# Attention with one-pass softmax: how the row-maximum units of a head group are dealt out over the score steps

## What is computed

```
c_kv   = x @ W_dkv.T                                   # 64 latent channels
q_lat  = einsum('bhtd,hdl->bhtl', q, k_eff)            # 16 heads
attn   = einsum('bhtl,bsl->bhts', q_lat, c_kv) / sqrt(16)
attn   = softmax(where(causal, attn, -inf))
y      = attn @ c_kv @ v_eff                           # 1024 x 256 per sequence
```

## Time and profile before

| | us |
|---|---|
| median of 3 executions (lowest, highest) | 1578.49 (1576.39, 1583.69) |
| the profiled execution | 1577.51 |
| its span, first to last instruction | 1575.1 |
| first scores of group 0 (TensorE) to the end of the attention | 189 to about 794 |

### The profile page before, as it was taken

How to read it: one execution, slowest core, us unless ns; L and a number is a source line. 1 busy time by engine, 2 the same in 40 slices (tenths; PEclk the granted TensorE clock), 3 DMA queues, 4 the chain that set the end, 5 groups by cost and what they waited for, 6 DMA issues and landing times. The chain is left out here.

```text
span 1575.1 us, 26764 instructions
## 1 busy us (share of the span) xinstructions
PE 1122.4 (71%) x8321; PEld 786.8 (50%) x8322; DVE 880.2 (56%) x2078; ACT 647.8 (41%) x1114; POOL 509.2 (32%) x490
## 2 busy tenths in 40 slices
PE   6835688888888888888814505978979979899000
PEld 3412344434443434444214405977979979899000
DVE  5514556655665666556058535666575675655245
ACT  3520155545554555555635422533433434344322
POOL 3100033323332333333446774033031230300785
PEclk9975578877887988778855556999989999899555
DMA  5964213221322132201111243121221212111324
GB/s 161 300 180 127 73 48 98 71 75 50 98 69 75 59 99 68 78 35 45 35 55 44 78 144 124 60 90 44 92 90 43 92 40 91 37 46 40 90 80 156
DMA packets 94507, 133.15 MB, mean 85 GB/s; under 512 B 26372, under 2 KB 68756, under 8 KB 94356
## 3 DMA queue, kind: packets, MB, share of 16 engines
q1 hardware_dynamic: 82696, 95.51, 19.7%
q0 software_dynamic: 11744, 36.74, 7.3%
HBM read 75.82 MB, written 55.87 MB: 84 GB/s over the span
## 5 line engine op out<-in xcount | busy, mean ns | idle before, releaser
L742 ACT ACTIVATE att_pt<-att_ps_s 128x1024 f32<-128x1024 f32 (+3 forms) x384 | 294.8, 812 | 269.8 <-PE att_ps_s L660 268.4
L772 DVE TENSOR_REDUCE att_pm<-att_ps_m 128x1 f32<-128x512 f32 (+1 forms) x512 | 306.6, 651 | 176.7 <-PE att_ps_m L612 104.5
L1409 ACT ACTIVATE moe_hf<-moe_ps_h,moe_b 128x256 f32<-128x256 f32 x288 | 136.9, 475 | 295.3 <-PE moe_ps_h L1360 241.4
L612 PE MATMUL att_ps_m<-att_k,att_q 50*128 50x512 f32 (+3 forms) x576 | 178.3, 449 | 20.8 <-DVE att_pm L772 10.7
L570 POOL TENSOR_SCALAR_AFFINE_SELECT att_pt<-att_pt 128x512 f32<-128x512 f32 x128 | 80.5, 635 | 325.1 <-ACT att_pt L742 325.1
L1435 DVE TENSOR_TENSOR moe_hTl<-moe_hf,moe_hTh 128x256 fp32r<-128x256 f32 x288 | 163.3, 567 | 9.9
L660 PE MATMUL att_ps_s<-att_q,att_k 50*128 50x512 f32 (+3 forms) x576 | 141.0, 451 | 31.8 <-ACT att_pt L742 30.9
L677 PE MATMUL att_ps_o<-att_pt,att_v 128*17 128x512 f32 (+3 forms) x1152 | 142.8, 618 | 10.1 <-POOL att_pt L570 6.2
L560 POOL TENSOR_TENSOR att_rec<-att_sums,att_minus 128x16 f32<-128x16 f32 x33 | 95.8, 2903 | 140.3 <-ACT att_sums L728 140.3
L1433 DVE CAST moe_hTh<-moe_hf 128x256 fp32r<-128x256 f32 x288 | 119.9, 416 | 33.7 <-ACT moe_hf L1409 33.6
L612 PEld LDWEIGHTS att_ps_m<-att_k,att_q 50*128 50x128 f32 x576 | 92.9, 217 | 66.2 <-DVE att_pm L772 49.9
(11 more groups left out here) (199 smaller groups left out, 2570.5 us busy)
## 6 DMA issues: line engine op xcount, KB each, us to landing
weights_raw<-in_w POOLq DMA_DIRECT2D x14, 1024.0 KB, 7.3
ys<-att_zeros SPq DMA_DIRECT2D x16, 640.0 KB, 3.7
moe_rows<-xs SPq DMA_DIRECT2D x38, 256.0 KB, 2.7
ys<-moe_o SPq DMA_DIRECT2D x36, 256.0 KB, 2.2
att_q<-qs SPq DMA_DIRECT2D x48, 128.0 KB
att_k<-ks SPq DMA_DIRECT2D x48, 128.0 KB
vs<-proj_v SPq DMA_DIRECT2D x32, 136.0 KB, 7.7
proj_x<-in_x POOLq DMA_DIRECT2D x8, 512.0 KB, 6.6
```

Of the source, the lines that this page charges most:

```text
L612: last[e] = pe.matmul(ps_m[(n + e) % NBK][:, at_col:end], qg[slot][rows, h // 2, i * P:(i + 1) * P], kg[slot][rows, h // 2, k0:k0 + keys], ...
L742: act.activation(pt[:, blk % NPT, 2 * p:2 * p + 2, off:CH], ps_s[k % 2][:, :, off:CH], ACT.Exp, scale=HS ** -0.5).then_inc(ex_done, 1)
L772: return dve.tensor_reduce(pm[:, g % 2, place, h:h + 1], src, AX.X, ALU.max)
L1409: act.activation(hf[:, f % NHB], ps_h[f % NHB][:], ACT.Relu, bias=b1[r][:, f:f + 1]).then_inc(hf_done, 1)
```

## The change

The units of a pair are no longer interleaved: each is one job of TensorE by itself, complete with its short matmuls and its report. The deal over the steps comes from a table (`EARLY`), and four units stand behind the values passes 1, 13, 17 and 21 (`LATE`) instead of ahead of them. The order of the units stays the same.

```diff
+EARLY = (2, 2, 3, 1, 1, 0, 2, 3, 2, 0, 2, 2, 1, 1, 1, 1, 2, 1, 2, 2, 1, 0, 1, 1)
+LATE = {1: 1, 13: 1, 17: 1, 21: 1}
 def bank_jobs():
-    work = [("unit", 1, m) for m in range(HALF, NU, 2)] + [("unit", 2, m) for m in range(0, HALF, 2)]
-    cost = [2 * unit_keys(m) + 128 for _, _, m in work]
-    width = [CH - max(0, (j - c * TC) * P) + 96 for c, j, _ in STEPS]
...
-        out[step] += [(kind, more, m), (kind, more, m + 1)]
+    work = [("unit", 1, m) for m in range(HALF, NU)] + [("unit", 2, m) for m in range(0, HALF)]
+    out, late, n = [], [], 0
+    for k, few in enumerate(EARLY):
+        more = LATE.get(k, 0)
+        out.append(work[n:n + few])
+        late.append(work[n + few:n + few + more])
+        n += few + more
     out[5] += [("out", 0, 0)]
     out[13] += [("out", 0, 1)]
     out[17] += [("turn", 1, 0), ("turn", 1, 1)]
-    return out
+    return [out[k] + [("values", 0, k)] * (k % 4 == 1) + late[k] for k in range(NS)]
...
-                def units(b, g, m, n):
...
-                            for e in range(2):
-                                h = UNITS[m + e][0][pair]
-                                rows = slice(64 * e, 64 * e + KM)
-                                if at_col == 0:
-                                    free(b, n + e)
-                                last[e] = pe.matmul(ps_m[(n + e) % NBK][:, at_col:end], qg[slot][rows, h // 2, i * P:(i + 1) * P],
...
-                            if diag:
-                                for z in range(2):
-                                    for e in range(2):
-                                        rows = slice(64 * e, 64 * e + 64)
...
-                    for e in range(2):
-                        last[e].then_inc(bank_made[(n + e) % NBK], 1)
+                def unit(b, g, m, n):
...
+                    free(b, n)
+                    end = 0
                     for i, k0, keys, _ in pieces:
+                        for h in heads:
                             diag = k0 + keys == (i + 1) * P
+                            at_col, end = end, end + keys
+                            ins = pe.matmul(bank[:, at_col:end], qg[slot][rows, h // 2, i * P:(i + 1) * P],
+                                            kg[slot][rows, h // 2, k0:k0 + keys], start=True, stop=not diag)
+                            for z in range(2 if diag else 0):
+                                col = end - P + z * (P // 2)
+                                ins = pe.matmul(bank[:, col:col + P // 2], pick[mask, z], future[mask, z],
+                                                start=False, stop=z == 1)
+                    ins.then_inc(bank_made[n % NBK], 1)
```

More of the change, by code:

```diff
@@ L409, in unit_keys @@
     return len(heads) * sum(keys for _, _, keys, _ in pieces)
+EARLY = (2, 2, 3, 1, 1, 0, 2, 3, 2, 0, 2, 2, 1, 1, 1, 1, 2, 1, 2, 2, 1, 0, 1, 1)
+LATE = {1: 1, 13: 1, 17: 1, 21: 1}
 def bank_jobs():
-    work = [("unit", 1, m) for m in range(HALF, NU, 2)] + [("unit", 2, m) for m in range(0, HALF, 2)]
-    cost = [2 * unit_keys(m) + 128 for _, _, m in work]
-    width = [CH - max(0, (j - c * TC) * P) + 96 for c, j, _ in STEPS]
[L419 to L422, removed]
-        out[step] += [(kind, more, m), (kind, more, m + 1)]
-        done += c
+    work = [("unit", 1, m) for m in range(HALF, NU)] + [("unit", 2, m) for m in range(0, HALF)]
[5 more added lines that the diff above has]
+        n += few + more
+    assert n == NU
     out[5] += [("out", 0, 0)]
@@ L427, in bank_jobs @@
     out[17] += [("turn", 1, 0), ("turn", 1, 1)]
-    return out
+    return [out[k] + [("values", 0, k)] * (k % 4 == 1) + late[k] for k in range(NS)]
 AFTER = bank_jobs()
-JOBS = sum(len(x) for x in AFTER)
+JOBS = sum(what[0] != "values" for x in AFTER for what in x)
 assert JOBS % NBK == 0 and NB % NPT == 0
@@ L490, in numbered @@
                 for k in range(NS):
-                    here = [j for j in AFTER[k] if ahead(b, g, j[1])]
-                    steps.append([(j, n + i) for i, j in enumerate(here)])
-                    n += len(here)
+                    here = []
+                    for j in AFTER[k]:
+                        if ahead(b, g, j[1]):
+                            here.append((j, n))
+                            n += j[0] != "values"
+                    steps.append(here)
                 out.append(steps)
@@ L594, in free @@
                         pe.wait_ge(bank_read[n % NBK], turns(b, n))
-                def units(b, g, m, n):
-                    pieces = UNITS[m][1]
-                    slot = g % NSL
+                def unit(b, g, m, n):
+                    heads, pieces = UNITS[m]
+                    slot, e = g % NSL, heads[0] % 2
+                    rows = slice(64 * e, 64 * e + KM)
+                    mask = slice(64 * e, 64 * e + 64)
+                    bank = ps_m[n % NBK]
                     if m == 0:
@@ L601, in units @@
                         pe.wait_ge(loaded[slot], at(b, g // NSL * NSL, LOADS, NSL * LOADS + ONES))
-                    at_col, last = 0, [None, None]
+                    free(b, n)
+                    end = 0
                     for i, k0, keys, _ in pieces:
-                        for pair in range(len(UNITS[m][0])):
+                        for h in heads:
                             diag = k0 + keys == (i + 1) * P
-                            end = at_col + keys
-                            for e in range(2):
-                                h = UNITS[m + e][0][pair]
-                                rows = slice(64 * e, 64 * e + KM)
-                                if at_col == 0:
-                                    free(b, n + e)
-                                last[e] = pe.matmul(ps_m[(n + e) % NBK][:, at_col:end], qg[slot][rows, h // 2, i * P:(i + 1) * P],
-                                                    kg[slot][rows, h // 2, k0:k0 + keys], start=True, stop=not diag)
-                            if diag:
-                                for z in range(2):
-                                    for e in range(2):
-                                        rows = slice(64 * e, 64 * e + 64)
[L618 to L621, removed]
@@ L642, in jobs @@
                         if kind == "unit":
-                            if m % 2 == 0:
-                                units(b, g + more, m, n)
+                            unit(b, g + more, m, n)
+                            continue
+                        if kind == "values":
+                            for blk in (m // 2 - 2, m // 2 - 1):
+                                if blk >= 0:
+                                    values(b, g, blk)
+                                elif g > 0:
+                                    values(b, g - 1, NB + blk)
                             continue
@@ L687, in body @@
                             jobs(b, g, steps[k])
[L688 to L693, removed]
                     for blk in (NB - 2, NB - 1):
```

## The result

The changed kernel takes 1621.7 us (median of 4, 1616.8 to 1631.4) beside 1577.4 us before (1573.8 to 1583.7): a ratio of 1.029, interval 1.025 to 1.033. It is 2.9% slower, where 1.8% faster was forecast, and outside the range. The profiled execution took 1617.5 us, its span is 1615.2.

What follows compares the result with a forecast made beforehand. TensorE was taken to bound the attention loop, its length set by holes in its queue and by the clock. 17 us from the deal plus 11 from the clock made 28 off 1577.5: 1550 us, range 1506 to 1590.

Steps and rivals of the forecast that it cites:

- The step that failed: Attention loop clock: shortening the longest stretch saves a fifth of the 3.9 us half-clock price, 0.8 a group, 11 in all.
- The sum at full clock: Six stretches between values passes: the new deal saves 1.2 us a group, 17 us over 14 groups.
- Lone units: Un-interleaved units on TensorE: 0.36 us more per single-diagonal pair, 0.88 for pair 0/1; 4.6 us a group if unhidden.
- Rival B: Diagonal units: un-interleaving costs more than the deal gives, 1.5 us a group, 21 in all, 1599 us; chance 0.18.
- Rival A: Attention loop: TensorE may hold full clock through most groups, down to 1506 us, likely near 1520; chance 0.22.
- Prologue and turn: The 58 first jobs before the loop, and the turn coming two units earlier in its stretch: both costed at nothing.

## Why the prediction was wrong

**The step that failed** is the one on the clock: "I take a fifth of the 3.9 us as saved, 0.8 a group, 11 us in all", with "as much lost again as 0.8" for its worst bound. Time at half clock rose from 218 to 333 us of the loop. The loop grew by 34 us although its stretches at full clock say it should have lost 14 x 1.84 = 26 (or 22 by the estimate of 1.6); so the 115 us more at half clock cost 56 to 60 us, about half a microsecond each. The argument behind the step was that the clock falls in the longest stretch without a pass, and that cutting it makes falls rarer. The first half was right for the kernel before, with 14 of 28 falls between passes 13 and 17. The second half failed: those went down to 5, but the falls in all rose to 42, and most of the new ones came in or next to 5 to 9 and 21 to 1, of 3.67 us each: shorter than the 4.00 and 4.84 us that the prediction had seen keep 1.00. Nor is the lower clock the deal's alone: lone units in the old deal had 0.78, an even deal of pairs 0.79, before 0.82. Nine identity matmuls a group raised the mean clock of even pairs from 0.79 to 0.95.

**The sum at full clock** was right in sign and, for five of the six stretches, within 0.2 us. Forecast and measured: 13 to 17, 4.1 and 4.04; 17 to 21, 3.15 and 3.02; 21 to 1, 3.5 and 3.66; 1 to 5, 3.85 and 3.69; 5 to 9, 3.66 and 3.67; 9 to 13, 5.1 and 4.62. 1.2 us a group forecast, 1.84 measured, most of the difference from 9 to 13. The prediction's own full-clock length of a group is a little too long, since the 6.93 us in it had a clock of 0.90.

**Lone units** were mis-sized at full clock. I took 0.36 us more for each pair with a diagonal. PE in order of time in the changed kernel, behind pass 9: lone units 35 and 36 with their short matmuls between two scores; then unit 0 alone, whose first matmul starts at 207.15, the fourth at 207.79.

```profile
205.81 0.39 PE L615 MATMUL att_ps_m<-att_k,att_q 50*128 50x512 f32 x2
206.04 0.23 PE L619 MATMUL att_ps_m<-keep_future,keep_pick 64*128 64x64 bf16 x4
206.11 0.48 PE L664 MATMUL att_ps_s<-slots_q,slots_k 50*128 50x512 f32 x2
...
207.15 0.29 PE L615 MATMUL att_ps_m<-att_k,att_q 50*128 50x128 f32 x1 [0.26 <-DVE att_pm L770]
...
207.79 0.30 PE L615 MATMUL att_ps_m<-att_k,att_q 50*128 50x128 f32 x1
207.80 0.49 PE L664 MATMUL att_ps_s<-slots_q,slots_k 50*128 50x512 f32 x1
207.94 0.23 PE L619 MATMUL att_ps_m<-keep_future,keep_pick 64*128 64x64 bf16 x2
208.01 0.48 PE L664 MATMUL att_ps_s<-slots_q,slots_k 50*128 50x512 f32 x1
```

Units 35 and 36 together take the 0.30 us that the interleaved pair took the earlier trace rows: in different halves of the array the second one starts beside the first. A unit with several pieces in its own half is slower alone, unit 0 with 0.21 to 0.22 us a piece, and there 0.88 us was right as its length. As a price it was too high: one score matmul of step 12 starts at 207.80, ahead of unit 0's last two short ones at 207.94, though the program has it behind them. It uses the other half of the array.

The 0.40 us that the prediction read as an odd unit alone hides the same thing. Between 554.99 and 555.39 of the kernel before stand

```profile
555.10 0.50 PE L660 MATMUL att_ps_s<-att_q,att_k 50*128 50x512 f32 x1
555.33 0.23 PE L619 MATMUL att_ps_m<-keep_future,keep_pick 64*128 64x64 bf16 x2
```

so the next score matmul had started in the other half 0.11 us behind the unit's, before the unit's own short ones.

**Rival B** had the side and the wrong mechanism. Its time, 1599, was that of TensorE's own work, 4.6 us a group for lone units; in the old deal they made one stretch 0.64 us longer at full clock and another 0.62 shorter, with nine identity matmuls added they cost 0.7%, and with ten the changed kernel is faster than before. The Trainium skill ("TensorE: Matmul & The Clock Gate", on packing small matmuls) says that loads for other rows overlap a running matmul; the pair 35/36 agrees. That matmuls start in strict order, which the prediction also took from the Trainium skill, doesn't hold for these rows: both times a matmul for one half started ahead of earlier ones for the other (207.80 ahead of 207.94, 555.10 ahead of 555.33). The rows decide.

**Rival A** took the fall's place for its cause. With the stream fed, the changed kernel is at 1539, in the forecast's range and still 19 us above the 1520 that this rival named. What it drew from the Trainium skill ("TensorE: Matmul & The Clock Gate", on HAM oscillation), that the clock is lost when the matmul stream pauses, agrees with the runs in which waits were filled (0.74 to 0.90); my reading of it, that an even deal is the cure, doesn't.

**What was not seen** is the price of the four late units, 1.7% between 1.012 and 1.029. The forecast costed the one behind pass 1 as 0.2 us of delay.

**Prologue and turn** were rightly costed at nearly nothing: the changed kernel's loop starts 1.2 us later, its first scores wait 13.1 us for the maxima's DMA, and no later group's wait for it is in its list of waits.

**Open:** why a lone unit, an evener deal, or a unit behind a pass lowers the clock at the same amount of work. Only that they do, and that work in the thin stretches undoes it, is shown. Part of the price of the late units may be that of the unit counts that moved with them.

## To carry to other kernels

Where the granted clock of a TensorE-bound loop has a mean between its levels, do the sum once for each level and count where the clock falls, before and after: here the added time at half clock cost 56 to 60 us, more than twice what the new order saved at full clock. In this kernel an evener order paid only with the thin stretches kept busy; a few matmuls that compute nothing, put where TensorE waits anyway, turned 2.9% slower into 2.4% faster, and with pairs kept into 3.2% faster. Put next to the dense work, the same matmuls cost 3%.

## What was unexpected

- More work made the loop shorter: 640 to 559 us with 150 matmuls more (300 as the profile counts), the mean clock 0.74 to 0.90.
- The falls of the clock moved to short stretches: 3.67 us long at full clock, with TensorE busy for over 90% of them.
- Six identity matmuls a group gave a clock of 0.91 and a ratio of 0.975, nine gave 0.95 and 0.968.
- Two lone units in different halves of the array take 0.30 us together with their six matmuls, no more than when interleaved, and a matmul for one half can start ahead of an earlier one for the other half.
